# Attention of a DiT block: row maxima turned by VectorE and spread by ScalarE, output gathered channel-major by DMA and divided there

## The chip, the cores and the metric

The kernel runs on one core of a Trainium2 chip. The metric is device microseconds of one execution, lower is better. The core has a matrix engine (TensorE, PE in the profile, with its weight loads as PEld), VectorE (DVE), ScalarE (ACT), GpSimd (POOL) and SyncE (SP), which here only issues the DMAs, in the order in which they are written.

## The reference

One transformer block with modulation, over 32 samples of 256 tokens and 288 channels, all in float32:

```python
B, L, C = 32, 256, 288;  H = 16;  D = C // H;  FF = 4 * C      # D = 18, FF = 1152
ada = silu(c) @ W_ada + b_ada                                  # six vectors per sample
h = layernorm(x) * (1 + scale_msa) + shift_msa
q, k, v = split(h @ W_qkv + b_qkv)
attn = softmax(einsum('blhd,bmhd->bhlm', q * D ** -0.5, k), axis=-1)
o = einsum('bhlm,bmhd->blhd', attn, v).reshape(b, l, c)
x = x + gate_msa * (o @ W_proj + b_proj)
h = layernorm(x) * (1 + scale_mlp) + shift_mlp
x = x + gate_mlp * (gelu(h @ W_fc1 + b_fc1) @ W_fc2 + b_fc2)
```

## The kernel before

All engines run a list of steps (`PE_ORDER`, `ACT_ORDER`, `DVE_ORDER`, `POOL_ORDER`, `SYNC_ORDER`). An entry `("st", 0, 3)` is step `st`, for the sample whose number is that of the row plus 0, with index 3. `run` (L106) goes through the list once per row, so that in the middle of the kernel a row does each step once, for samples of different ages: the MLP works on sample k-2, the projection on k-1, the scores on k, the next QKV on k+1. The order is written out; semaphores set only how long a step waits. One row is one sample's worth of work, and there are 32 samples.

Precision: a float32 operand is split into a rounded part (`fp32r`) and a rest, and three products replace one. With 288 channels that is 7 matmuls for each output tile (`products`, L296).

Attention works in pairs of heads, 8 pairs a sample, 4 pairs a half:

- `qk` (L462) makes q and k, channels by tokens. ACT and DVE write the rounded part and the rest to `qst`. SP writes `qst` to DRAM (`qkw`, L365) and reads it back, 18 rows at a time, into `ql` and `kl` (`qkr`, L376, 24 reads a sample), which lines up high and low parts as one contraction of 108 rows.
- `s` (L484) computes the scores, tokens by keys, into two banks; DVE takes the row maxima (`head_max`, L814) and puts them into `mx`.
- `mt` (L502) turns the maxima of two pairs on PE (2 transposes); ACT copies four rows to `mxs` (L637); SP sends them to rows 108 and 109 of `ql` with 2 DMAs (`mx_out`, L396).
- `st` (L511) computes the scores again, keys by tokens, over 110 rows: the two extra rows subtract the maximum. 4 matmuls of 256 columns. ACT takes the exponential into `e` (L642).
- `pv` (L523), once per four heads (a quad), multiplies `e` with `ve`, 18 channels of v and a one for the sum per head. The result is channels by tokens, in four groups of 32 partitions. ACT copies it to `ots` (L650), `on` (L535) turns it on PE to tokens by channels, and DVE takes the reciprocal of the sums and multiplies (L823) into `onat`.
- `ot` (L541) turns `onat` on PE back to channels by tokens (6 transposes), ACT and DVE split it into `xh3`, `xl3`, `xr3`, and `proj` (L546) does the projection.

`lt`, `fc1`, `fc2`, `sum2` and the layer norms are the same before and after. POOL computes rests (`xl1`, `xl3`, `gl`) and additions. `xt` and `lt` are the PE transposes after the layer norms; they stay.

Of the kernel before, what the change touches and what calls it, by code (L numbers as in the profile page):

```python
# [26 lines left out]
KH = 2 * KS  # L27
KM = KH + 2
# [14 lines left out]
GROUPS = 4  # L43
MXW = 64 + 4 * GROUPS
READS = 8
# [3 lines left out]
A_USES = 2 + NT + 2 + 3  # L49
USE_PROJ, USE_LT, USE_FC1 = 2, 2 + NT, 4 + NT  # L50
B_USES = 2 + NT
USE_FC2 = 2
TURN_USES = 2 * QUADS
# [29 lines left out]

POOL_ORDER = [
    ("fc1", -2, 2), ("fc1", -2, 3), ("xt", 2, 0), ("fc1", -2, 4), ("proj", -1, 0), ("proj", -1, 1),
    ("ln2_stats", -1, 0), ("lt", -1, 0), ("sum2", -2, 0), ("bias", -1, 0), ("ln1_stats", 3, 0), ("sum2", -2, 1),
    ("fc1", -1, 0), ("fc1", -1, 1),
]

# [908 lines left out]
```

## Time and profile before

| | us |
|---|---|
| median of 3 runs | 1330.55 (1329.88 to 1333.33) |
| the profiled execution | 1333.92, its span 1332.1 |

| engine | busy us | share | instructions |
|---|---|---|---|
| PE | 1283.3 | 96% | 10995 |
| PEld | 1160.8 | 87% | 10995 |
| DVE | 884.9 | 66% | 2086 |
| ACT | 714.0 | 54% | 1163 |
| POOL | 480.2 | 36% | 522 |

Busy time counts an instruction from its start to its end. PE's instructions overlap, so what one of them costs is the distance from its start to the next one's start, which the chain of waits shows. The DMA engines were busy for about a third of the span. The first 120 us load weights and fill the pipeline of samples; the last 60 us drain it.

### The profile page before, as it was taken

The page shows a single profiled execution, that of the slowest core. Times are in us where ns is not written, and L with a number is a line of the kernel's source. Part 1 is how long each engine was busy: PE and PEld are TensorE (multiplying, and loading weights), DVE is VectorE, ACT ScalarE, POOL GpSimd, SP SyncE. Part 2 cuts the span into 40 slices and gives each one's busy share as a digit, 9 for nine tenths or more (in the row PEclk, how much of TensorE's full clock was granted, in tenths as well). Part 3 has the DMA queues.
Part 4 walks back from the last instruction along what each step waited for, and adds up shares of the span by engine and source line. Part 5 has one row for each costly group of instructions (what it writes and reads, how often), then busy time and mean ns, then how long its engine had stood idle before and what let it go on. Part 6 is the DMA issues. An engine that isn't in the chain of part 4 may idle for free.

```text
span 1332.1 us, 29243 instructions
## 1 busy us (share of the span) xinstructions
PE 1283.3 (96%) x10995; PEld 1160.8 (87%) x10995; DVE 884.9 (66%) x2086; ACT 714.0 (54%) x1163; POOL 480.2 (36%) x522
## 2 busy tenths in 40 slices
PE   6588999999999999999999999999999999999996
PEld 1477999999999999999999999999999999999886
DVE  5567666667667666666766667676667666766642
ACT  1345556556555555655556555555655555565541
POOL 2102343333334333333343333334333433433344
PEclk9998999999999999999999999999999999999998
DMA  7234333333333333433334343333424333332210
GB/s 233 87 122 136 103 109 112 105 116 122 115 115 103 108 115 105 127 112 116 106 103 125 95 130 112 117 103 105 124 92 131 112 119 108 101 114 85 82 47 18
DMA packets 82934, 146.27 MB, mean 110 GB/s; under 512 B 12486, under 2 KB 51496, under 8 KB 82796
## 3 DMA queue, kind: packets, MB, share of 16 engines
q1 hardware_dynamic: 82796, 144.40, 34.7%
q8 instruction: 90, 1.47, 0.5%
q14 instruction: 48, 0.39, 0.1%
HBM read 96.53 MB, written 47.30 MB: 108 GB/s over the span
## 4 chain that ended last, share of the span: by engine, by line
PE 94%; DVE 3%; ACT 1%; issue 1%; DMA 1%; POOL 0%; SPq 0%; POOLq 0%; ACTq 0%; DVEq 0%
PE x_bank L472 11%; PE a_bank L571 10%; PE turn_bank L530 9%; PE score_bank L497 9%; PE st_bank L519 9%; PE b_bank L571 8%; PE b_bank L585 6%; PE b_bank L587 6%; PE b_bank L586 6%; PE a_bank L552 5%; PE x_bank L480 5%; PE score_bank L507 2%; PE a_bank L450 2%; PE turn_bank L538 2%; PE x_bank L450 1%; PE a_bank L453 1%
## 5 line engine op out<-in xcount | busy, mean ns | idle before, releaser
L819 DVE TENSOR_REDUCE mx<-score_bank 128x2 f32<-128x512 f32 x512 | 337.9, 687 | 201.8 <-PE score_bank L497 199.4
L646 ACT ACTIVATE e<-st_bank 128x1024 f32<-128x1024 f32 x256 | 262.7, 1026 | 116.2 <-PE st_bank L519 112.1
L948 POOL TENSOR_TENSOR gl<-gl_raw,gh 128x512 fp32r<-128x512 f32 (+1 forms) x160 | 188.6, 1179 | 182.6 <-DVE gh L877 182.6
L585 PE MATMUL b_bank<-w,gh 128*128 128x288 f32 x576 | 176.5, 306 | 0.7 <-DVE tmp L883 0.6
L497 PE MATMUL score_bank<-kl,ql 108*128 108x256 f32 x1024 | 172.2, 290 | 1.1 <-ACT mxs L640 1.0
L519 PE MATMUL st_bank<-ql,kl 110*128 110x256 f32 x1024 | 170.2, 288 | 0.5 <-ACT e L646 0.5
L587 PE MATMUL b_bank<-w,gl 128*128 128x288 f32 x576 | 170.5, 296 | 0.0
L586 PE MATMUL b_bank<-w,gh 128*128 128x288 f32 x576 | 170.3, 296 | 0.0
L497 PEld LDWEIGHTS score_bank<-kl,ql 108*128 108x128 f32 x1024 | 142.1, 192 | 14.6 <-issue 14.5
L519 PEld LDWEIGHTS st_bank<-ql,kl 110*128 110x128 f32 x1024 | 140.5, 190 | 5.0 <-issue 1.3
L530 PE MATMUL turn_bank<-e,ve 128*32 128x256 f32 x2048 | 137.0, 385 | 0.1
L935 POOL TENSOR_TENSOR xl<-v,xh 128x512 fp32r<-128x512 f32 x32 | 41.3, 1292 | 213.7 <-DVE xh L869 213.7
L472 PE MATMUL x_bank<-xh,wq 128*128 128x256 f32 x640 | 106.8, 291 | 6.8 <-DVE qst L808 3.7
L585 PEld LDWEIGHTS b_bank<-w,gh 128*128 128x128 f32 x576 | 109.1, 189 | 1.3 <-DVE tmp L883 0.9
L571 PE MATMUL a_bank<-xh,w 128*128 128x256 f32 x640 | 105.7, 287 | 4.1 <-DVE xr L795 2.9
L586 PEld LDWEIGHTS b_bank<-w,gh 128*128 128x128 f32 x576 | 109.4, 190 | 0.0
L587 PEld LDWEIGHTS b_bank<-w,gl 128*128 128x128 f32 x576 | 108.8, 189 | 0.0
L627 ACT CAST qst<-x_bank 128x512 fp32r<-128x512 f32 (+1 forms) x96 | 49.3, 514 | 110.4 <-PE x_bank L472 109.6
L472 PEld LDWEIGHTS x_bank<-xh,wq 128*128 128x128 f32 x640 | 91.7, 198 | 8.5 <-issue 7.3
L640 ACT CAST mxs<-score_bank 4x256 fp32r<-4x256 f32 x128 | 46.5, 363 | 94.3 <-PE score_bank L507 92.6
L571 PEld LDWEIGHTS a_bank<-xh,w 128*128 128x128 f32 x640 | 88.0, 190 | 5.8 <-issue 5.8
L877 DVE CAST gh<-gl_raw 128x512 fp32r<-128x512 f32 (+1 forms) x160 | 85.3, 533 | 11.5 <-ACT gl_raw L679 11.4
(153 smaller groups left out, 2597.6 us busy)
## 6 DMA issues: line engine op xcount, KB each, us to landing
qk_rows<-qst SPq DMA_DIRECT2D x128, 256.0 KB, 2.5
ql<-qk_rows SPq DMA_DIRECT2D x384, 72.0 KB
kl<-qk_rows SPq DMA_DIRECT2D x384, 72.0 KB
gate<-gates SPq DMA_DIRECT2D x32, 432.0 KB, 4.7
xin<-in_x SPq DMA_DIRECT2D x32, 288.0 KB, 3.0
x<-in_x SPq DMA_DIRECT2D x32, 288.0 KB, 3.2
out<-x SPq DMA_DIRECT2D x32, 288.0 KB, 3.1
qk_rows<-qst SPq DMA_DIRECT2D x32, 128.0 KB, 4.7
```

What stands on the lines that cost most here:

```text
L472: last = nc.tensor.matmul(x_bank[:, k * L:(k + 1) * L], wa[:, c * P:(c + 1) * P], xa, start=(i == 0), stop=(i == len(pr) - 1))
L497: last = nc.tensor.matmul(score_bank[i][:, t * L:(t + 1) * L], ql[0:KH, slot, i, j % HP, t * P:(t + 1) * P], kl[0:KH, slot, j % HP, :], st ...
L519: last = nc.tensor.matmul(st_bank[:, i, u, :], kl[0:KM, slot, j % HP, u * P:(u + 1) * P], ql[0:KM, slot, i, j % HP, :], start=True, stop=True)
L530: last = nc.tensor.matmul(turn_bank[VB * c:VB * (c + 1), 0:L], ve[:, b % 2, u, 4 * q + c, :], e[:, 2 * (q % 2) + c // 2, c % 2, u, :], sta ...
L571: last = nc.tensor.matmul(bank[:, (f % 2) * L:(f % 2 + 1) * L], wa[:, f * P:(f + 1) * P], xa, start=(i == 0), stop=(i == len(pr) - 1))
L585: nc.tensor.matmul(b_bank[:, 0:C], gh[:, cols], w2[:, 0, f, :], start=(f == 0), stop=False)
L586: nc.tensor.matmul(b_bank[:, 0:C], gh[:, cols], w2[:, 1, f, :], start=False, stop=False)
L587: last = nc.tensor.matmul(b_bank[:, 0:C], gl[:, cols], w2[:, 0, f, :], start=False, stop=(f == NF - 1))
L646: nc.scalar.activation(e[:, j % 4, :, :, :].rearrange("p i u l -> p (i u l)"), st_bank[:, :, :, :].rearrange("p i u l -> p (i u l)"), ACT. ...
L819: nc.vector.tensor_reduce(mx[:, b % 2, :, col:col + 1], score_bank[i][:, :].rearrange("p (t l) -> p t l", t=NT), AX.X, ALU.max).then_inc(s ...
L877: nc.vector.tensor_copy(gh[:, cols], g[:, cols]).then_inc(g_hi, 1)
L948: nc.gpsimd.tensor_tensor(gl[:, cols], g[:, cols], gh[:, cols].bitcast(F32), ALU.subtract).then_inc(g_lo, 1)
```

## The change

The change takes three kinds of PE transposes away and moves their work to DVE, ACT and DMA.

- **Maxima.** DVE writes the maxima of four pairs (a half) so that its own transpose in blocks of 32 (`mt`, now on DVE) puts them into rows. ACT then spreads them with 8 copies of 4 partitions (`mb`) straight into rows 64 to 67 of `ql`. `kl` has a -1 in the row of the pair concerned and 0 in the others. The two reads of zeros a sample (`qkr` with `m == 12`) clear these rows of `ql` before `s`, which now contracts over the same 122 rows as `st`. `mt` on PE, the copy to `mxs` and the 8 DMAs of `mx_out` go.
- **Scores, keys by tokens.** `st` uses 2 matmuls of 512 columns in place of 4 of 256.
- **Output.** `pv` is done once per eight heads. ACT copies both quads' results to `on` in one go; SP writes them to DRAM (`ow`, 4 DMAs) and reads them back as packed channels (`or`, 6 DMAs), 7 heads in each of two tiles and 2 heads in a third. The sums go on their own: gathered over 64 partitions (`sr`, 2), reciprocal on DVE (`rcp`), out to DRAM (`sw`, 2), read back repeated 18 times (`rr`, 6). DVE multiplies (`om`), ACT rounds (`oh`), POOL and DVE take the rest (`ol`), `proj` contracts over 126 rows. `on` and `ot` on PE go.
- The five lists are written anew.

The core of the diff (`...` marks what is left out):

```diff
 def st(b, j):
-    if j % 2 == 0:
-        pe.wait_ge(mx_rows[gr % 2], 32 * (2 * b + gr // 2 + 1))
+    if j % HP == 0:
+        pe.wait_ge(mx_rows, HALVES * b + j // HP + 1)
     wait(pe, e_ready, PAIRS * b + j)
-    for i in range(2):
-        for u in range(NT):
-            last = nc.tensor.matmul(st_bank[:, i, u, :], kl[0:KM, slot, j % HP, u * P:(u + 1) * P],
-                                    ql[0:KM, slot, i, j % HP, :], start=True, stop=True)
+    for u in range(NT):
+        last = nc.tensor.matmul(st_bank[:, u, :, :], kl[0:KM, slot, j % HP, u * P:(u + 1) * P],
+                                ql[0:KM, slot, :, j % HP, :], start=True, stop=True)
...
-def mt(b, gr):                       # PE: 2 transposes, 4 times a sample
-def on(b, q):                        # PE: 2 transposes, 4 times a sample
-def ot(b, n):                        # PE: 4 and 2 transposes, once a sample
...
+def mb(b, half):                     # ACT
+    act.wait_ge(mx_turned, HALVES * b + half + 1)
+    rows = ql[MXR:MXR + HP, slot, :, :, :].rearrange("p i j (t a x) -> p i j t a x", t=NT, x=VB)
+    for t in range(NT):
+        for a in range(P // VB):
+            src = mxt[VB * a:VB * a + HP, half, :, t, :].unsqueeze(2).broadcast_to([HP, 2, HP, VB])
+            last = nc.scalar.copy(rows[:, :, :, t, a, :], src)
+    last.then_inc(mx_rows, 1)
...
+def mt(b, half):                     # DVE
+    for i in range(2):
+        dve.wait_ge(s_max[i], PAIRS * b + HP * (half + 1))
+    wait(dve, mx_rows, HALVES * (b - 1) + half + 1)
+    nc.vector.transpose(mxt[:, half].rearrange("p i t v -> p (i t v)"),
+                        mx[:, half].rearrange("p i t v -> p (i t v)")).then_inc(mx_turned, 1)
+def rcp(b, half):                    # DVE
+    dve.wait_ge(sums_loaded[half], 16 * (b + 1))
+    wait(dve, rc_stored[half], 16 * b)
+    nc.vector.reciprocal(rc[part, :], sums[part, :]).then_inc(rc_ready, 1)
...
+def sum_read(b, half):               # SP
+    sp.wait_ge(turn_drained, HALVES * b + half + 1)
+    sp.dma_start(sums[P // 2 * half:P // 2 * (half + 1), :], ...).then_inc(sums_loaded[half], 16)
+def rc_write(b, half):
+    sp.wait_ge(rc_ready, HALVES * b + half + 1)
+    sp.dma_start(r_dram[b % 2, half]..., rc[...]).then_inc(rc_stored[half], 16)
...
 def proj(b, t):
-    pe.wait_ge(a_drained, A_USES * b + USE_PROJ + t)
-    pr = products(xh3, xl3, xr3, wp)
+    pe.wait_ge(o_lo, b + 1)
+    pe.wait_ge(o_rem, b + 1)
+    wait(pe, a_drained, A_USES * b + USE_PROJ + t)
+    pr = products(oh, ol, orem, wp, OT, OREM)
```

How the order moves, at the places that matter. First PE, in the middle of a row. Before, around the end of the MLP's first layer and the start of the second (`L538` is `on`, `L507` `mt`, `L450` `ot` and `xt`):

```order
L571 MATMUL b_bank<-xr,w 128x256
L538 MATMUL turn_bank<-ident,ots 128x128 x2
L507 MATMUL score_bank<-ident,mx 68x128 x2
L571 MATMUL a_bank<-xh,w 128x256 x4
L571 MATMUL a_bank<-xl,w 128x256 x2
L571 MATMUL a_bank<-xr,w 128x256
```

and now, with `L655` for `fc1`, `L610` for `st` and `L599` for `s`:

```order
L655 MATMUL b_bank<-xr,w 128x256
L655 MATMUL a_bank<-xh,w 128x256 x4
L655 MATMUL a_bank<-xl,w 128x256 x2
L655 MATMUL a_bank<-xr,w 128x256
L610 MATMUL st_bank<-ql,kl 128x512 x2
L599 MATMUL score_bank<-kl,ql 128x256 x4
```

The transposes between the blocks of `fc1` are gone, all five blocks of `fc1` are issued before the row's first `st`, and an `st` is 2 instructions.

Second ACT, at the exponentials after the GELUs. Before (`L657` and `L659` are `ot`, `L652` `pv`, `L640` `mt`):

```order
L646 ACT_TABLE_LOAD
L646 ACTIVATE e<-st_bank 128x1024
L657 CAST xh<-a_bank 128x512
L618 ACTIVATE v<-x_bank,mod 128x256 x2
L659 CAST xr<-a_bank 96x256
L646 ACTIVATE e<-st_bank 128x1024
L652 COPY ots<-turn_bank 128x256
L640 CAST mxs<-score_bank 4x256
```

Now the later half of a row, from the fourth exponential on (`L738` is `st`, `L731` `mb`, `L720` `v`, `L748` `pv`):

```order
L738 ACTIVATE e<-st_bank 128x1024
L731 CAST ql<-mxt 4x8x32 x8
L720 COPY ve<-x_bank 128x16x18
L748 COPY on<-turn_bank 128x512
L738 ACTIVATE e<-st_bank 128x1024
L702 ACTIVATE xl_raw<-x_bank,mod 128x256 x2
```

The small copies come in two blocks of 8, and the copy of the `pv` result stands behind such a block.

Third SP's queue, over the stretch in which the output goes out and comes back. Before it held the reads of q and k and the maxima:

```order
L392 DMA kl<-qk_rows 18x1024
L402 DMA ql<-mxs 1x2x256 x2
L392 DMA kl<-qk_rows 18x1024 x2
L373 DMA qk_rows<-qst 128x2x256 x2
L392 DMA ql<-qk_rows 18x1024 x5
L402 DMA ql<-mxs 1x2x256 x2
```

Now (`L460` is `sw`, `L451` `sr`, `L445` `ow`, `L494` `or`, `L481` `rr`, `L407` `qkw`, `L435` `qkr`):

```order
L460 DMA r_rows<-rc 64x32
L451 DMA sums<-on 64x1x32
L445 DMA o_rows<-on 4x32x256 x2
L383 DMA xin<-in_x 128x576
L494 DMA ol_raw<-o_rows 126x1x256
L498 DMA out<-x 128x576
L481 DMA rcb<-r_rows 126x1x256
L407 DMA qk_rows<-qst 128x2x256
L460 DMA r_rows<-rc 64x32
L494 DMA ol_raw<-o_rows 126x1x256
L494 DMA orem_raw<-o_rows 36x1x256 x2
```

The writes and reads of the output and of the sums stand between the reads of q and k of one sample and the writes of q and k of the next, and the queue waits for a reciprocal of DVE twice in a row. A row issues 55 DMAs, where it issued 41.

## Rows read from the trace of the kernel before

**Rows 1.** The page: busy time of each engine, and the chain's shares by engine.

```profile
PE 1283.3 (96%) x10995; PEld 1160.8 (87%) x10995; DVE 884.9 (66%) x2086; ACT 714.0 (54%) x1163; POOL 480.2 (36%) x522
...
PE 94%; DVE 3%; ACT 1%; issue 1%; DMA 1%; POOL 0%; SPq 0%; POOLq 0%; ACTq 0%; DVEq 0%
```

**Rows 2.** Stretches: length, busy PE, PEld, DVE, ACT, POOL, clock, DMA share, GB/s.

```profile
200.00:1250.00 1050.00, 1049.70 (x9286) 965.08 (x9278) 722.88 (x1727) 599.16 (x977) 396.08 (x431) 1.00 0.36 112
...
1200.00:1238.70 38.70, 38.70 (x343) 35.54 (x343) 24.48 (x55) 20.54 (x33) 12.58 (x13) 1.00 0.33 105
...
1290.00:1310.00 20.00, 13.87 (x91) 12.75 (x90) 8.79 (x23) 3.52 (x7) 8.95 (x10) 0.91 0.00 1
```

**Rows 3.** The chain of waits over one row: start us, us, what.

```profile
601.23 0.48 PE score_bank L497 x4
601.70 1.00 PE turn_bank L530 x16
602.70 1.12 PE x_bank L480 x7
603.83 1.65 PE a_bank L571 x14
...
606.44 0.93 PE x_bank L480 x7
...
609.04 0.22 PE turn_bank L538 x2
...
610.45 0.13 PE b_bank L586
...
611.99 0.44 PE a_bank L450 x4
...
615.01 0.22 PE a_bank L453 x2
...
640.39 1.00 PE turn_bank L530 x16
```

**Rows 4.** Groups by line (two stretches): busy, mean ns of one, idle before.

```profile
L640 ACT CAST mxs<-score_bank 4x256 fp32r<-4x256 f32 x128 | 46.5, 363 | 94.3 <-PE score_bank L507 92.6
...
L652 ACT COPY ots<-turn_bank 128x256 f32<-128x256 f32 x42 | 15.7, 373 | 4.1 <-PE turn_bank L530 4.1
...
L657 ACT CAST xh<-a_bank 128x512 fp32r<-128x512 f32 x11 | 6.4, 582 | 0.0
...
L842 DVE TENSOR_TENSOR xl<-a_bank,xh 128x512 fp32r<-128x512 f32 x11 | 7.6, 691 | 3.9 <-ACT xh L657 3.9
...
L827 DVE RECIPROCAL rc<-turn_bank 128x8 f32<-128x8 f32 x42 | 8.4, 201 | 9.5 <-PE turn_bank L538 9.5
...
L830 DVE TENSOR_TENSOR onat<-turn_bank,rc 128x144 f32<-128x144 f32 x43 | 13.2, 307 | 1.5
...
L930 POOL TENSOR_TENSOR xl<-v,xh 128x512 fp32r<-128x512 f32 x11 | 14.1, 1283 | 34.7 <-DVE xh L800 34.7
```

**Rows 5.** SP's issues in order of time: start us, us, what, count.

```profile
612.54 0.43 SPq L362 DMA_DIRECT2D gate<-gates  x1
...
613.40 1.07 SPq L373 DMA_DIRECT2D qk_rows<-qst  x2
...
623.02 1.23 SPq L402 DMA_DIRECT2D ql<-mxs  x2
...
629.36 0.78 SPq L392 DMA_DIRECT2D kl<-qk_rows  x2
630.19 2.46 SPq L373 DMA_DIRECT2D qk_rows<-qst  x2
```

**Rows 6.** The page: DMA issues, KB each, median us to landing.

```profile
qk_rows<-qst SPq DMA_DIRECT2D x128, 256.0 KB, 2.5
...
qk_rows<-qst SPq DMA_DIRECT2D x32, 128.0 KB, 4.7
```

**Rows 7.** SP's waits from 600 to 1010 us: us in total, times, longest.

```profile
SPq L382 <- DMA qk_rows<-qst: 62.8, 21, 4.9
```

More of the change, by code:

```diff
@@ L26 @@
 KS = 3 * D
-KH = 2 * KS
-KM = KH + 2
+MXR = 64
+HB = MXR + PAIRS // 2
+KM = HB + KS
 VB = 32
@@ L260, in dit_block @@
                                      (w_fc1, b_fc1, w1, w1_raw, FF)):
+            rows, rem = (OT, OREM) if w is w_proj else (P, KRB)
             for k in range(2):
-                loads.append(("full", w, None, raw[:, 2 + k, :], dst[:, k, :], dst[:, 2 + k, :], n, k))
-            loads.append(("rem", w, bias, g[0:KRB, at:at + n], dst[0:KRB, 4, :], None, n, 2))
+                loads.append(("full", w, None, raw[0:rows, 2 + k, :], dst[0:rows, k, :], dst[0:rows, 2 + k, :], n, k))
+            loads.append(("rem", w, bias, g[0:rem, at:at + n], dst[0:rem, 4, :], None, n, 2))
+            if w is w_proj:
+                wp_rem_raw = g[:, at:at + n]
             at += n
@@ new lines, in sum_read @@
+            def sum_read(b, half):
+                wait(sp, rc_ready, HALVES * (b - 1) + half + 1)
+                sp.wait_ge(turn_drained, HALVES * b + half + 1)
+                sp.dma_start(sums[P // 2 * half:P // 2 * (half + 1), :],
+                             on_sb[D:P:VB, :, :].rearrange("c q l -> c (q l)").rearrange("c (x i) -> c x i", i=VB)
+                             ).then_inc(sums_loaded[half], 16)
+            def rc_write(b, half):
+                sp.wait_ge(rc_ready, HALVES * b + half + 1)
+                if half == 0 and b >= 2:
+                    sp.wait_ge(rc_rows[b % 2], 16 * O_READS * (b // 2))
+                sp.dma_start(r_dram[b % 2, half].rearrange("c q (x i) -> (c q x) i", i=VB),
+                             rc[P // 2 * half:P // 2 * (half + 1), :]).then_inc(rc_stored[half], 16)
@@ new lines, in o_read @@
+            def o_read(b, n):
+                if n == 0:
+                    wait(sp, a_full, A_USES * (b - 1) + USE_PROJ + NT)
+                    sp.wait_ge(o_stored[0], 32 * (b + 1))
+                    if b == 0:
+                        sp.wait_ge(consts, N_CONSTS - 1)
+                if n == 1:
+                    sp.wait_ge(o_stored[1], 32 * (b + 1))
+                to, h0, nh = o_place(ol_raw, orem_raw, n)
+                heads = o_dram[b % 2].rearrange("f c q v l -> (f c q) v l")[:, 0:D, :]
+                sp.dma_start(to, heads[h0:h0 + nh]).then_inc(o_rows[b % 2], 16)
@@ L411, in _ @@
                 load_weights(i)
+            sp.wait_ge(consts, N_CONSTS - 1)
+            for jj in range(HP):
+                row = slice(MXR + jj, MXR + jj + 1)
+                sp.dma_start(kl[row, :, jj, :].bitcast(F32),
+                             tmp2[row, 0, 0:L].unsqueeze(1).broadcast_to([1, SLOTS, L])).then_inc(kl_rows, 16)
+            sp.dma_start(zero_dram, ql[MXR:MXR + HP, 0, :, :, :].rearrange("p i j l -> p (i j l)").bitcast(F32)
+                         ).then_inc(zeros_stored, 16)
             fetch_x(1)
@@ L499, in s @@
                                                 start=True, stop=True)
                     last.then_inc(s_full[i], 1)
-            def mt(b, gr):
-                for i in range(2):
-                    pe.wait_ge(s_max[i], PAIRS * b + 2 * gr + 2)
-                for t in range(NT):
-                    last = nc.tensor.transpose(mt_ps[0:68, t * P:(t + 1) * P],
-                                               mx[:, b % 2, t, 4 * gr:4 * gr + 68], ident[:, :])
-                last.then_inc(mt_full, 1)
@@ new lines, in st, with pv @@
+                last.then_inc(st_full, 1)
+            def pv(b, half):
+                pe.wait_ge(e_ready, PAIRS * b + HP * (half + 1))
+                if half == 0:
+                    pe.wait_ge(x_drained, X_USES * (b + 1))
+                wait(pe, turn_drained, HALVES * b + half)
+                for q in range(2):
+                    for u in range(NT):
+                        for c in range(4):
+                            last = nc.tensor.matmul(turn_bank[VB * c:VB * (c + 1), q * L:(q + 1) * L],
+                                                    ve[:, b % 2, u, 8 * half + 2 * c + q, :],
+                                                    e[:, c, u, q, :],
+                                                    start=(u == 0), stop=(u == NT - 1))
+                last.then_inc(turn_full, 1)
@@ L839, in ot @@
-            def ot(b, n):
-                dve.wait_ge(o_hi, 2 * b + n + 1)
+            def mt(b, half):
[7 more added lines that the diff above has]
+                wait(dve, rc_stored[half], 16 * b)
+                part = slice(P // 2 * half, P // 2 * (half + 1))
+                nc.vector.reciprocal(rc[part, :], sums[part, :]).then_inc(rc_ready, 1)
```

305 lines of the change are left out of this document (179 added, 126 removed), and 34 rows, old and new, of tables (ACT_ORDER, DVE_ORDER, PE_ORDER, POOL_ORDER).

## The prediction

> **What bounds the kernel now.** I read the page's busy times first, then the stretches, then the chain of waits over one row, and last the groups of the engines that take over the work. The page says PE 96% and a chain that runs 94% through PE [rows 1]. The stretches say where: from 200 to 1250 us PE is busy for 1049.70 of 1050 us at full granted clock, and only near the end does it leave gaps (13.87 of 20 us, clock 0.91) [rows 2]. DVE is busy there for 722.88/1050 = 69% and ACT for 57%. So the middle is one engine deep, and what a step costs there is its share of PE's time.
>
> A busy PE need not be a full one, so I take the chain's own distances. The first quad's `pv` of one row starts at 601.70 and the same step of the next row at 640.39: a row is 38.69 us [rows 3]. Its steps add up to that. `s` and `st` are 8 each at 0.48 = 7.7. `pv` is 4 at 1.00, and the block behind it takes 1.12 where the same block elsewhere takes 0.93, so 4 x 1.19 = 4.8. `qk` is 2.5 x 1.66 = 4.15, `v` and `proj` 4 x 0.93 = 3.7, `fc1` 4.5 x 1.66 = 7.5, `fc2` 54 x 0.133 = 7.2 (its row is rounded to 0.13; 288 columns against 256 at 0.119 give 0.133). `mt` is 4 x 0.22, `on` 4 x 0.22, and `ot`, `xt`, `lt` are 0.44 + 0.22 each. Sum 38.8, against 38.69: no idle time is left over, and a removed PE step gives its full price.
>
> The Trainium skill would read this otherwise: its page Perfetto Trace Analysis (Identifying the Most-Contended Engine) holds that busy matmuls say little and that the busy share of the weight loads is the measure. Here that is 87% [rows 1], and by it about an eighth of PE's time would be slack. But a block of 7 with 288 columns takes 0.93 and one with 256 takes 1.65/2 = 0.83, with weights of the same width [rows 3], so the moving columns set the pace; by this the trace does not agree.
>
> **What the change removes on PE.** Per row: 8 transposes of `mt`, 8 of `on`, 6 of `ot`, each 0.11: 22 x 0.11 = 2.42 us. `pv` comes in 2 pieces instead of 4, and two of the four slow starts behind it go: 2 x 0.19 = 0.38. `st` streams as many columns with half as many instructions. Nothing, if time goes by columns; at most the fixed part of 16 matmuls, which I bound by 0.119 less 256 columns at 2.4 GHz (0.107) = 0.012 each, 0.2 us. The rows at 256 and 288 columns (0.119, 0.133) lie nearer to pure proportion, so I take 0.1. `s` and `proj` contract over other numbers of rows; `s` at 108 and `st` at 110 rows cost the same 0.48, as do blocks with a remainder of 98 rows, so that is 0. In all 2.9 us, and the row's floor is 35.8 us (bounds 35.7 to 35.9).
>
> **What it adds elsewhere.** ACT is at 0.57 x 38.69 = 22.1 us a row. It loses 4 x 0.363 + 4 x 0.373 + 0.58 + 0.37 = 3.9 and gains 16 small copies, 2 copies of 512 columns at 0.58, and 0.58 + 0.37 for the rounding [rows 4]. The small copies are the nearest thing to L640 (4 partitions, 256 elements, 363 ns): 5.8 us, bounded by 0.2 each, for an instruction that only starts (as the small reciprocal), and 0.58, for one of 512 columns, so 3.2 to 9.3. ACT comes to 26 us (24 to 30) of 35.8. DVE is at 26.6; it loses about 3.5 (`on` 4 x 0.51, `ot` 1.1, small copies 0.4) and gains 2 transposes of 128 elements (between 0.2 and 0.69, I take 0.3, near L830), 2 reciprocals at about 0.3, 0.69 + 0.42 for the product and 0.42 for the rest: 25.8. POOL gains 1.28. None of them becomes the bound by its sum.
>
> SP issues 55 DMAs a row instead of 41. At the prices of [rows 5]: 26 reads at 0.39, 5 writes of q and k at 0.53 to 1.23 (0.8), 4 others at 0.43, 4 small ones at 0.61, 4 writes of the output at 0.53, 12 reads at 0.43: 10.1 + 4.0 + 1.7 + 2.4 + 2.1 + 5.2 = 25.5 us, where it was 20. To this come two waits a row for landed q and k, 62.8/21 = 3.0 each [rows 7]: 31.5 of 35.8. The DMA engines carry 1.3 MB more in a row on top of 4.5 MB (144.40 MB over 32): the share goes from 0.36 [rows 2] to about 0.36 x 1.3 x 38.7/35.8 = 0.51.
>
> **The paths that have to fit.** All in PE time between the steps, by [rows 3].
> - From `s` 7 to `st` 4 stand 2 `v`, 2 `proj`, one `st`, one `pv` of eight heads: 4 x 0.93 + 0.46 + 2.19 = 6.4 us. Needed: two maxima 1.4, transpose 0.3, 8 copies 2.9 = 4.6. Slack 1.8. The same for the first half: 8.0 against 4.6.
> - From `pv` of the second half to `proj`: 5 blocks of `fc1`, 3 of `qk`, 6 `s`, 4 `st`, 2 parts of `fc2`, 1 `v`: 19.8 us. Needed: copy 0.6, three DMA legs (issue 0.6 + landing 2.5 [rows 6], again 3.1, six reads 2.6 + 2.5), reciprocal 0.3, product 0.7, rounding 0.6, POOL 1.3 = 14.8. Slack 5. With landings of 4.7 each it is 21.4, 1.6 too long.
> - From `qk` 1 to the next sample's `s` 0: 19.7 us. Needed: cast and rest 1.3, about 3 of queueing on ACT behind `mb` and the GELUs, two writes 2.5, landing 2.5, 13 reads 5.1, landing 2.5 = 16.9. Slack 2.8. Before, this path had most of a row more.
>
> The Trainium skill, DMA: Bandwidth & Descriptors (Anatomy of one DMA), puts about 2.0 us on a small DMA, most of it the receipt of the last write, most of all into HBM. This estimate would make the three legs 6 us plus issues, and the middle path about 13 us; no row here shows a transfer of so few bytes landing.
>
> DVE's queue also waits now for DMA: `rcp` stands ahead of the third maximum of a sample, so late sums hold `s` back.
>
> I expect the slacks to hold mostly, with 0.4 us of PE waits a row (bounds 0 and the 1.6 above). Row: 36.2, a gain of 2.5 us over 31 full rows = 77 us. **The ends** cost something: in the drain only about 7.5 + 2.4 = 9.9 us of MLP lie between the last `pv` and its `proj`, for a path of 14.8, so 5 us of idle PE; at the start four pairs instead of two must be scored before the first `st`, 1 us. Plus 6 (0 to 12). Span 1332.1 - 77 + 6 = 1261. The profiled execution took 1333.92, 1.8 over its span and 3.4 over the median, so **1260 us** against 1330.55.
>
> **The rivals.**
> - *Waits take half of the gain.* One of the three paths is late in each row, most likely q and k or the output, since both pass SP's queue. At the 1.6 us worked out above the row is 37.4, the gain 31 x 1.3 = 40 us: 1295. For it: slacks of 2 to 5 us against landings that already vary from 2.5 to 4.7. Against: PE is in order, so a late row shifts the others along and the slack grows back.
> - *SP's queue becomes the bound, and the kernel is slower.* The place is the stretch of output and sum DMAs. The 22 new issues have prices from 0.39 to 1.23 (the write pair at 630.19). The rest of SP's row is 15.1 plus 6 of waits, so the queue binds from 0.67 us per new issue, and decides for slower from (38.7 - 21.1)/22 = 0.80. At 0.9 a row is 40.9, 2.2 longer: 1330 + 68 + 6 = 1405 us. For it: the same write took 0.53 in one place and 1.23 in another, so issues slow when the queue is full, and each of the new waits (for a reciprocal, for landed sums) stops all reads behind it. Against: reads are issued at 0.39 to 0.43.
> - *PE is not what the gain is paid in.* If the freed time is only refilled with waits on the scores (DVE's maxima at 0.69 each follow every `s`), the row stays at 38.7: 1333. DVE's 69% speaks against it.
> - *Everything hides*, ends too: 35.7 x 31 gives a gain of 93, 1237.
>
> **Chances.** Forecast (1243 to 1275) 0.62; waits take part (1275 to 1320) 0.20; everything hides (below 1243) 0.06; row unchanged 0.03; SP bound, slower 0.09. A measurement of this kernel can tell about 0.3%, 4 us, from no change: faster 0.88, same 0.02, slower 0.10. The range 1240 to 1305 leaves out about 0.03 below and 0.15 above.
>
> **What would show it.** Right: the `pv` of one half starts about 36.2 us after the same one in the row before; PE busy for over 98% of the middle at full clock; no group of transposes but `xt` and `lt`; small copies near 0.36; ACT near 26 and DVE near 26 us a row. Wrong: PE idle before `proj`, `s` or `st` in sum over 1 us a row, put down to POOL `ol`, to the DMAs into `ql`, or to ACT's copies; SP issuing without a pause; `rcp` on DVE waiting for `sums` with maxima queued behind it; 1.2 GHz stretches in the middle.

## The result: 1.8% slower, and the profile after

The changed kernel takes 1354.91 us (median of 4 runs, 1351.16 to 1361.93) against 1330.56 of before in the same comparison (1329.88 to 1333.33): a ratio of 1.018, 95% interval 1.015 to 1.021. The forecast was 1260 with a range to 1305, so both the sign and the range were wrong. The profiled execution has a span of 1350.1 us, against 1332.1.

The page of the changed kernel, as in [rows 1] busy time by engine and the chain's shares by engine and by line:

```profile
PE 1227.3 (91%) x9779; PEld 1081.7 (80%) x9779; DVE 940.7 (70%) x1929; ACT 871.3 (65%) x1483; POOL 530.6 (39%) x557
...
PE 29%; issue 17%; DMA 17%; SPq 13%; POOL 12%; DVE 7%; ACT 4%; POOLq 0%; DVEq 0%; ACTq 0%
```

PE did become lighter: 1227.3 us busy instead of 1283.3, 1216 instructions fewer. But the chain that was 94% PE is now 29% PE. Its largest line is `DMA r_rows<-rc 10%`, a transfer of 8 KB: the reciprocals on their way to DRAM.

Where the time lies is best seen between the stores of the output. I cut both traces at the store of the first sample and at that of the 28th, 27 rows apart. The first row here is before, the second after (columns as in [rows 2]):

```profile
176.54:1221.18 1044.64, 1044.64 (x9242) 961.14 (x9238) 720.75 (x1725) 596.25 (x973) 395.48 (x430) 1.00 0.36 112
```

```profile
185.04:1225.87 1040.83, 992.12 (x8204) 891.37 (x8203) 770.80 (x1588) 727.87 (x1242) 437.94 (x457) 0.99 0.48 147
```

| stretch | before | after | difference | foreseen |
|---|---|---|---|---|
| to the first store | 176.5 | 185.0 | +8.5 | about +1 |
| 27 rows | 1044.6 | 1040.8 | -3.8 | -67.5 |
| from there to the end | 110.9 | 124.2 | +13.3 | -10 (four rows) +5 |

A row went from 38.69 to 38.55 us. So what PE gave back was eaten in the row itself, and the two ends made the kernel slower. PE's busy time fell by 52.5 us over the 27 rows (1.94 a row) and 48.7 us of idle time came in its place (1.80 a row). PE's waits in that stretch, total us, times, longest:

```profile
PE st_bank L610 <- ACT e L738: 41.4, 27, 2.5
PE a_bank L636 <- DVE tmp L964: 3.2, 3, 1.7
```

It is one wait, exactly once in each of the 27 rows: `st` for its bank, which ACT's exponential empties. The prediction had idle time before `st` among its signs of being wrong, but put it down to ACT's copies of the maxima, not to an exponential. The other engines' waits tell what stands behind it; ACT, DVE and SP's queue in turn:

```profile
ACT oh L754 <- DVE ol_raw L946: 58.6, 27, 3.1
```

```profile
DVE rc L939 <- DMA sums<-on: 56.8, 27, 3.7
...
DVE ol_raw L946 <- DMA rcb_rem<-r_rows: 47.8, 27, 2.7
```

```profile
SPq L416 <- DMA qk_rows<-qst: 117.7, 52, 5.4
SPq L450 <- ACT on L748: 59.7, 27, 3.5
SPq L498 <- POOL x L1077: 33.6, 28, 2.7
SPq L481 <- DMA r_rows<-rc: 26.9, 25, 2.2
```

All occur about once or twice a row. (The wait of `rc` for the sums is that of the first half's reciprocal, at 604.82 in the row below; the second half's, at 611.77, starts without a wait.) The chain over one row puts them in order (start us, us, what; the eight heads' `pv` had ended at 607.86, and the copy L748 ran from 607.93 to 608.52):

```profile
611.78 0.78 POOL x L1077
...
612.57 0.36 SPq L498
...
613.03 0.82 SPq L481
...
613.95 0.47 SPq L407
...
614.49 4.57 DMA r_rows<-rc
...
619.07 0.79 SPq L481
...
621.70 0.77 SPq L481
...
622.52 2.38 DMA rcb_rem<-r_rows
...
624.92 0.70 DVE ol_raw L946
...
625.64 0.03 ACT oh L754
...
626.17 1.03 ACT e L738
...
627.24 0.74 PE st_bank L610 x2
...
628.46 1.76 PE x_bank L582 x7
```

Read from below. PE's `st` at 627.24 waits for the exponential at 626.17. That one is late though its scores were there at 624.2: in ACT's list `oh(-1,0)` stands ahead of it, and `oh` waits for the product of the output with the reciprocals. The product waits for the last of the reads of reciprocals, those for the landing of the write of the reciprocals, and that write was issued only at 614.49 although the reciprocals were there at 612.12: it stands in SP's queue behind a store, a read and a write of q and k. The store itself waited for POOL's last addition of the MLP until 612.56, 0.4 us longer than the reciprocals took; this is the branch that the profile's chain follows, and where its 12% of POOL come from. Both branches go back to PE at nearly the same place. The sums come from `pv` (605.93 to 607.86), and `pv` of a second half needs the exponentials. POOL's addition stands in POOL's list behind work on the transposes of `lt`, a step just ahead of that `pv` in PE's list (605.62). So the loop is closed. One row is once around it, and PE only runs along. The last line shows the rest of the price: behind the gap the block of 7 that takes 0.93 in [rows 3] takes 1.76. The granted clock of that stretch (its column is the third from the right) is half of full speed, the level of 1.2 GHz, after 1.84 us in which PE had stood still:

```profile
628.30:630.30 2.00, 2.00 (x10) 2.00 (x9) 1.82 (x4) 0.95 (x2) 0.00 (x0) 0.53 0.73 281
...
632.00:634.00 2.00, 2.00 (x16) 1.99 (x16) 0.66 (x2) 1.93 (x6) 0.87 (x2) 1.00 0.70 197
```

### The profile page after: what moved, and what is told of

The parts are those of the page before. It is cut to its first block, busy times and chain, and to the rows that moved or that the text cites. A ratio compares the mean times of both kernels' runs of the same rounds, so it can differ in the third digit from the quotient of the medians.

```text
span 1350.1 us, 27363 instructions
## 1 busy us (share of the span) xinstructions
PE 1227.3 (91%) x9779; PEld 1081.7 (80%) x9779; DVE 940.7 (70%) x1929; ACT 871.3 (65%) x1483; POOL 530.6 (39%) x557
## 4 chain that ended last, share of the span: by engine, by line
PE 29%; issue 17%; DMA 17%; SPq 13%; POOL 12%; DVE 7%; ACT 4%; POOLq 0%; DVEq 0%; ACTq 0%
DMA r_rows<-rc 10%; SPq L481 9%; PE st_bank L610 5%; PE turn_bank L622 5%; PE a_bank L636 5%; DMA rcb_rem<-r_rows 5%; PE x_bank L582 4%; POOL x L1071 3%; POOL xl L1042 3%; POOL xl L1047 3%; ACT e L738 2%; DMA gate<-gates 2%; SPq L494 2%; POOL x L1077 2%; SPq L407 2%
## 5 line engine op out<-in xcount | busy, mean ns | idle before, releaser
L922 DVE TENSOR_REDUCE mx<-score_bank 128x2 f32<-128x512 f32 x512 | 331.7, 680 | 60.8 <-PE score_bank L599 57.4
L738 ACT ACTIVATE e<-st_bank 128x1024 f32<-128x1024 f32 x256 | 262.1, 1024 | 52.4 <-PE st_bank L610 46.2
L610 PE MATMUL st_bank<-ql,kl 122*128 122x512 f32 x512 | 178.4, 430 | 60.1 <-ACT e L738 54.8
L731 ACT CAST ql<-mxt 4x256 fp32r<-4x256 f32 x512 | 206.2, 403 | 12.0 <-DVE mxt L931 5.2
L599 PEld LDWEIGHTS score_bank<-kl,ql 122*128 122x128 f32 x1024 | 154.4, 196 | 28.3 <-issue 11.3
L599 PE MATMUL score_bank<-kl,ql 122*128 122x256 f32 x1024 | 173.9, 293 | 2.1 <-DVE mx L922 1.9
L610 PEld LDWEIGHTS st_bank<-ql,kl 122*128 122x128 f32 x512 | 81.8, 196 | 86.2 <-ACT e L738 65.6
L622 PE MATMUL turn_bank<-e,ve 128*32 128x256 f32 x2048 | 125.3, 386 | 0.7 <-ACT e L738 0.7
L1047 POOL TENSOR_TENSOR xl<-xl_raw,xh 128x512 fp32r<-128x512 f32 x32 | 41.3, 1290 | 198.4 <-DVE xh L977 198.4
L1059 POOL TENSOR_TENSOR x<-tmp,x 128x288 f32<-128x288 f32 x64 | 51.3, 802 | 157.6 <-DVE tmp L964 157.6
L655 PE MATMUL a_bank<-xh,w 128*128 128x256 f32 x640 | 104.5, 285 | 8.4 <-DVE xr L898 3.9
L655 PEld LDWEIGHTS a_bank<-xh,w 128*128 128x128 f32 x640 | 88.3, 191 | 12.0 <-issue 6.1
L622 PEld LDWEIGHTS turn_bank<-e,ve 128*32 128x32 f32 x2048 | 60.4, 110 | 46.0 <-issue 11.6
```

Source lines behind the costliest of these rows:

```text
L599: last = nc.tensor.matmul(score_bank[i][:, t * L:(t + 1) * L], ql[0:KM, slot, i, j % HP, t * P:(t + 1) * P], kl[0:KM, slot, j % HP, :], st ...
L610: last = nc.tensor.matmul(st_bank[:, u, :, :], kl[0:KM, slot, j % HP, u * P:(u + 1) * P], ql[0:KM, slot, :, j % HP, :], start=True, stop=True)
L622: last = nc.tensor.matmul(turn_bank[VB * c:VB * (c + 1), q * L:(q + 1) * L], ve[:, b % 2, u, 8 * half + 2 * c + q, :], e[:, c, u, q, :], s ...
L655: last = nc.tensor.matmul(bank[:, (f % 2) * L:(f % 2 + 1) * L], wa[:, f * P:(f + 1) * P], xa, start=(i == 0), stop=(i == len(pr) - 1))
L731: last = nc.scalar.copy(rows[:, :, :, t, a, :], src)
L738: nc.scalar.activation(e[:, j % 4, :, :, :].rearrange("p u i l -> p (u i l)"), st_bank[:, :, :, :].rearrange("p u i l -> p (u i l)"), ACT. ...
```

## The experiments

Each kernel is the changed one with the edit shown, unless it says otherwise. Rows and waits are taken between the second and the 27th store, 25 rows. Times are set against the kernel before, run on the same chip.

**e1: the write of the second half's reciprocals goes ahead of the store.**

```diff
-    ("or", -1, 0), ("store", -3, 0), ("rr", -1, 0), ("qkw", 1, 0), ("sw", -1, 1), ("or", -1, 1),
+    ("or", -1, 0), ("sw", -1, 1), ("store", -3, 0), ("rr", -1, 0), ("qkw", 1, 0), ("or", -1, 1),
```

> Only SP's list changes: the DMA that writes the second half's reciprocals to DRAM (sw) stands ahead of the store of an older sample and of one read and one write, behind which it was issued at 614.49 though the reciprocal was ready at 612.12. Theory A (the output's way through SP and DRAM is what is too long: it ends in a rounding copy on ACT that stands in front of the second exponential, and PE waits for that exponential 1.5 us a row, and runs slow after it): the way gets about 2 us shorter, the wait for the exponential goes below 0.3 us a row, the clock in the middle rises to 1.00, a row goes from 38.55 to 36.0 to 36.9 us, the time from 1355 to 1290 to 1312. Rival B (ACT with 70% load and the copies of the maxima is itself what is late, the output's way only waits beside it): the row stays over 38.0, the time over 1338.

Measured: 1327.62 us, ratio 0.997 (0.995 to 0.999), row 37.59, between the bands of the two theories. One entry of SP's list is worth 1.0 us a row and 27 us of the whole. The wait of `st` fell only from 1.5 to 1.22 us a row, and the chain of this kernel has another last link:

```profile
631.26 5.35 DMA o_rows<-on
636.63 0.78 SPq L494
...
639.33 0.78 SPq L481
```

The write of 128 KB of output takes 5.35 us to land, and the ten reads behind it take 6.8 us to issue (636.63 to 643.45).

**e2: the reads of the divisor wait for nothing.** They fetch rows of x, so the divisor is another. (The wait for `rc_stored[1]` goes too.)

```diff
-                    sp.wait_ge(rc_stored[0], 16 * (b + 1))
-                src = r_dram[b % 2].rearrange(...)[h0:h0 + nh].unsqueeze(1)...
+                src = x[b, h0:h0 + nh, 0:L].unsqueeze(1)...
```

> The six reads of the reciprocals (rr) read rows of the input x of the same size and do not wait for the reciprocals to be in DRAM; the sums are still gathered, inverted and written. The division is by other numbers, so the output is not the reference's. Theory A: the two legs of the sums fall out of the way to the product, the wait for the second exponential goes to 0, a row is 36.0 to 36.6 us, the time 1285 to 1300, and the drain at the end is shorter by some 5 us of its 13 us excess. Rival B: the row stays over 38.0, the time over 1335.

Measured: 1331.85 us, ratio 1.000 (0.998 to 1.001), row 37.85, wait of `st` 1.26 a row. That is between the two theories again: taking the whole trip of the reciprocals away brings no more than issuing it in time did in e1. The branches of the loop are nearly equally long; below one lies the other. In some rows the chain of this trace goes through the landing of the output (5.42 us from 480.66). In others it has no landing but the last: the store waits for POOL's last addition until 634.03, and the ten reads behind it go out one after the other from 636.39 to 643.35.

**e3: the `oh` copies stand one exponential later in ACT's list.**

```diff
-    ("oh", -1, 0), ("st", 0, 1), ("qk", 1, 2), ("oh", -1, 1), ("st", 0, 2), ("v", 1, 0), ...
+    ("st", 0, 1), ("qk", 1, 2), ("oh", -1, 0), ("st", 0, 2), ("oh", -1, 1), ("v", 1, 0), ...
```

> Only ACT's list changes: the two rounding copies of the output (oh) stand one exponential later each. Theory A: the output's way is as long as before (product at about 24.9 us of a row that begins at 600), but the second exponential no longer waits; the wait moves in part to the projection, about 1 us a row. A row of 37.0 to 38.0 us, the time 1312 to 1340. If the wait for the exponential is only a symptom and the projection is as late as before, the whole comes back there: 1350 to 1360.

Measured: 1345.86 us, ratio 1.011 (1.006 to 1.015), row 38.40. The wait for the exponential is gone from PE's list and the row is hardly shorter. (The profiled execution, 1352.0 us, was the longest of the four; by the medians e3 is 9 us shorter than the changed kernel.) PE's new waits, and the largest of its weight loads (PEld):

```profile
PE x_bank L582 <- DVE qst L911: 14.5, 18, 1.3
PE score_bank L599 <- DVE mx L922: 5.5, 11, 1.0
```

```profile
PEld score_bank L599 <- DVE mx L922: 19.1, 40, 1.4
```

DVE's list has the same knot as ACT's: the product that waits for the DMA stands ahead of maxima and of `qst`, so its lateness reaches PE by that way. These waits are about half of the old one (20.0 of 37.5 us in 25 rows); another 12 are in PE's own busy time, 930.9 us where it was 919.0. Mostly it is the late product that costs, not the engine that hands it on.

**e4: the maxima are spread by 4 copies of 512 elements a half instead of 8 of 256.**

```diff
-                for t in range(NT):
-                    for a in range(P // VB):
-                        src = mxt[VB * a:VB * a + HP, half, :, t, :].unsqueeze(2).broadcast_to([HP, 2, HP, VB])
+                for a in range(P // VB):
+                    src = mxt[VB * a:VB * a + HP, half, :, :, :].unsqueeze(2).broadcast_to([HP, 2, HP, NT, VB])
```

> The maxima are spread by 4 copies of 512 elements for each half instead of 8 of 256. At 0.58 each (the cast of 512 columns) 2.4 us for 3.3, so ACT has 1.8 us less a row. Theory A: ACT's first exponential is at most 1 us earlier, but the second still waits for the output, whose way has no such copy in it; the copy of the second pv of a row is not moved: 38.0 to 38.6 us a row, 1340 to 1357. Rival B: ACT is what is late, the row falls by 1 us or more, 1320 or less.

Measured: 1343.66 us, ratio 1.009 (1.006 to 1.012), row 38.45. ACT got 1.5 us a row lighter (674.6 us over 25 rows in the changed kernel, 637.8 here), the row 0.1 shorter, and `st` waits as long as before (38.0 us in 25 rows, 37.5 in the changed kernel). So ACT's load is not what holds the row. It is not quite nothing: the medians are 11 us apart, 0.8%, the two intervals do not overlap, and the profiled execution (1350.12) was the longest of seven, so its row hides some of that.

**e5: nothing of the trip is waited for.** Output and divisor are both read from rows of x; the writes, the gather of the sums and the reciprocals still run. (The waits for the other half go too.)

```diff
-                    sp.wait_ge(rc_stored[0], 16 * (b + 1))
-                    sp.wait_ge(o_stored[0], 32 * (b + 1))
-                heads = o_dram[b % 2].rearrange("f c q v l -> (f c q) v l")[:, 0:D, :]
+                heads = x[b, 0:D * nh, 0:L].rearrange("(h v) l -> h v l", v=D)
```

> The changed kernel, but the reads of the output's rows and of the reciprocals' rows fetch rows of x instead and wait for nothing written in the same sample (the writes, the gather of the sums and the reciprocals still run), so what is multiplied is other data. Theory A (the kernel loses its gain in one loop: copy of the second half, trip through DRAM, product, oh copy ahead of the second exponential): nothing in this trip is waited for any more, so the wait of st for the second exponential (1.53 us a row in the changed kernel) goes to under 0.3, and with it the slow restart behind it (0.9); row 35.8 to 36.6 against 38.55; the drain rows, which were the trip itself, get 2 to 3 us shorter each; time 1265 to 1300. Rival B (SP's queue or DVE's own load sets the row, whatever the trip does): row 37.5 or more, since issues and DVE work are as many; the wait moves to score_bank or x_bank. Rival C (the middle recovers but the start keeps +8.5 us): the row as A, the first store still near 180.

Measured: 1294.38 us, ratio 0.971 (0.969 to 0.974), row 36.78. Stretch and PE's largest wait:

```profile
216.11:1135.51 919.40, 910.18 (x7602) 818.09 (x7601) 716.49 (x1476) 675.96 (x1150) 406.74 (x425) 1.00 0.51 155
```

```profile
PE st_bank L606 <- ACT e L734: 3.8, 5, 1.2
```

As many DMAs and as much DVE work as in the changed kernel, and 1.8 us a row less: the loss sits in the trip, not in the number of DMAs. Not all of the 1.8 is waiting, though. The reads of x also cost SP less to issue than those of the output (medians 0.55 and 0.36 us, where it was 0.79 and 0.53), some 1.2 us a row, and most of these reads stand in the same trip. e8 below reaches the same row, 36.78, with the reads at their old price and two more DMAs, so dearer reads need not cost it. The row came out 0.2 above the expected band. PE itself is busy for 910.18/25 = 36.4 us a row, and that, not a wait, is the missing part: my floor of 35.8 was too low. In the changed kernel it was 36.75, so the slow restarts cost about 0.35 a row. The first store is at 179.4 instead of 185.0, so 5.7 of the 8.5 us at the start were the same loop; from the 28th store to the end it still takes 121.3.

**e6: wide writes, on top of e1.** Heads are placed so that one write covers 128 whole rows in DRAM; the sums are gathered by two DMAs a half.

```diff
-                sp.dma_start(o_dram[b % 2, half, :, q], on_sb[:, q, :]).then_inc(o_stored[half], 16)
+                sp.dma_start(o_dram[b % 2, half, q].rearrange("c v l -> (c v) l"), on_sb[:, q, :]).then_inc(...)
```

> On top of e1 (sw ahead of the store). The heads of a half lie in DRAM so that each write of the output covers 128 whole rows of one block instead of 4 x 32 rows with gaps; the sums are gathered by two DMAs a half instead of one. Theory A (the write of the output is slow, 5.35 us, for its shape: 4 x 32 x 256 goes over 4 engines, 128 rows over 16): it lands in about 3 us; om comes 2 us earlier, the wait for the second exponential falls from 1.22 to 0.2 to 0.5 a row, row 36.3 to 37.2 against 37.59, time 1295 to 1318. Rival B (the landing is a receipt in DRAM or queueing behind other traffic, which a wider write does not shorten): landing stays above 4.5, row 37.6, and two more issues a row cost 0 to 0.5 us: 1325 to 1335. Rival C (the path through the sums and reciprocals is then the last one): landing falls, row only 37.3 or so, and om waits for rcb_rem behind rr reads.

Measured: 1304.18 us, ratio 0.979 (0.976 to 0.983), row 37.08, `st`'s wait 17.1 us in 25 rows. That is inside theory A's range, with a longer wait than it had (0.68 us a row). The same 128 KB now land in 1.9 us in the median (the line has min, median, max):

```profile
DMA to landing us min/median/max: 1.7/1.9/4.8
```

More issues a row, and a shorter row: rival B is out. Rival C is half right, since the chain now ends in the reads of the reciprocals again (the landing at 711.21, behind reads issued from 705.07 on). No landing stands between the reciprocals and it any more: from 702.34 to 711.21 SP issues 13 DMAs one after the other, 8.9 us. The price of an issue is itself a part of the loop.

```profile
702.34 0.52 SPq L461
...
705.07 0.79 SPq L495
...
711.21 2.24 DMA rcb_rem<-r_rows
713.47 0.70 DVE ol_raw L947
```

**e7: two semaphores, on top of e1.** The reads into the main tiles signal their own and go first.

```diff
-    ("or", -1, 1), ("or", -1, 2), ("or", -1, 3), ("or", -1, 4), ("rr", -1, 1), ("rr", -1, 2), ...
+    ("or", -1, 1), ("or", -1, 2), ("rr", -1, 1), ("or", -1, 3), ("or", -1, 4), ("rr", -1, 2), ...
-                sp.dma_start(to, src).then_inc(rc_rows[b % 2], 16)
+                sp.dma_start(to, src).then_inc((rc_rows if n < 2 else rc_rest)[b % 2], 16)
```

> On top of e1. The reads of the output and of the reciprocals signal two semaphores, one for the part in the main tiles and one for the rest, and the ones of the main part are issued first; om of the main tiles waits for its own only. Theory A (om waits 6 us for nine reads issued one after the other, of which it needs three): om and the oh copies come 2 to 4 us earlier, the wait for the second exponential goes under 0.4 a row, row 36.2 to 37.0 against 37.59, time 1290 to 1312. Rival B (the second product, of the rest, holds oh(1) or DVE instead): the wait moves to oh(1) and the third exponential, row 37.4 or more, 1322 to 1335.

Measured: 1317.34 us, ratio 0.989 (0.985 to 0.992), row 37.43. The row is rival B's, the time between the two: the wait for the exponential is gone altogether (30.5 us in 25 rows in e1), but 12.4 us come back at the bank of `proj`, and PE's busy time is 8.4 us longer, which no run explains.

```profile
PE a_bank L640 <- DVE tmp L970: 12.4, 15, 1.9
```

**e8: e1, e6 and e7 together.**

> e1, e6 and e7 together. Theory A (one loop, whose parts add up): the second exponential is never late, row 35.9 to 36.6, time 1278 to 1300, faster than before by 2 to 4%. Rival B (below about 37 us something else binds: DVE at 28.6 us a row with its in-order waits, or SP's queue with two more issues): row 36.8 to 37.4, not better than the better one of e6 and e7, and the idle time of PE is put to score_bank or x_bank.

Measured: 1283.69 us, ratio 0.965 (0.961 to 0.969), faster than before by 3.5%, in theory A's range. e1 brought 27 us over the changed kernel, e6 another 23, and the split wait, worth 10 on top of e1, another 20 on top of e6: what one cure brings depends on what the others have left. The profiled execution was the longest of the four (1292.5 us); its row is 36.78. No exponential is waited for, and nearly all of PE's idle time is `PE a_bank L641 <- DVE tmp L971: 11.0, 12, 2.0`, where DVE waits for the gates:

```profile
DVE tmp L971 <- DMA gate<-gates: 24.1, 17, 2.8
```

**e9: the load of residual and gates ahead of three writes of q and k, on top of e8.**

```diff
-    ("rr", -1, 5), ("qkw", 1, 1), ("qkw", 1, 2), ("qkw", 1, 3), ("res", -1, 0), ("qkr", 1, 0), ...
+    ("rr", -1, 5), ("res", -1, 0), ("qkw", 1, 1), ("qkw", 1, 2), ("qkw", 1, 3), ("qkr", 1, 0), ...
```

> On top of e8: the load of the residual and the gates goes ahead of the last three writes of q and k instead of behind them. In e8 the only wait of PE left in the middle is proj's second half for the bank, held by DVE's product with the gates (0.44 us a row), and DVE waited there for the gates. Theory A: that wait goes, the row falls from 36.75 to 36.3 (PE's own work), time 1268 to 1278. Rival B: the q and k writes come 1 us later and s waits for the kl rows instead, row 36.7 or more, 1283 or more.

Measured: 1339.35 us, ratio 1.005 (1.003 to 1.008), row 38.27. Theory A was right about the gates and wrong about the row: rival B, and stronger than I had thought. Some 0.9 us of issues moved (0.47 and 0.42 below) cost 1.5 us a row.

```profile
PE score_bank L604 <- DMA ql<-zeros: 43.1, 25, 4.3
PE a_bank L641 <- DVE tmp L971: 0.6, 1, 0.6
```

Its chain over a row is the second loop of this kernel, through the third path of the prediction:

```profile
605.21 1.24 DVE mx L927 x2
...
607.25 0.36 DVE rc L944
607.63 0.52 SPq L465
...
617.31 0.47 SPq L397
617.83 0.42 SPq L398
...
618.77 4.72 DMA qk_rows<-qst
623.61 0.30 SPq L437
...
627.90 4.38 DMA ql<-zeros
632.32 0.74 PE score_bank L604 x4
```

A maximum, the reciprocal that is queued behind it on DVE, the write of reciprocals on SP, ten reads, the two loads, the write of q and k and its landing of 4.72 us behind 720 KB of loads (the 256 KB writes landed in 4.6 us in the median, in e8 in 3.1), twelve reads, the scores, and 10 us of PE's and DVE's lists up to the next such maximum at 642.66. The output's reads and the reads of q and k share one queue, so what is issued or waited for on behalf of the one holds the other.

**e10: e9 with e4's four copies.**

> On top of e9: the maxima are spread by 4 copies of 512 elements a half instead of 8 of 256, which took 1.5 us a row off ACT in e4. Theory A (with the loop's path short enough, ACT at 27 of 36.3 us a row limits nothing): row as in e9 within 0.15; start and end together 0 to 3 us shorter; ratio to e9 within 0.4%. Rival B (ACT's queue still delays an exponential or the maxima here and there, as 37.5 us of waits in 25 rows did in the changed kernel): row 0.3 us shorter than e9.

Measured: 1334.74 us, ratio 1.002 (0.999 to 1.005), row 38.09. A row 0.18 us shorter and 0.3% of the whole, between the two theories in the row and within what the two intervals tell apart. ACT's load limits little in this loop too.

**e11: e9 with the write of the reciprocals back behind the store.**

> e9 with the write of the second half's reciprocals back behind the store, the first reciprocal read and a q/k write, where the changed kernel has it. Theory A (a loop: the write of the reciprocals was the last link only while it was issued 2 us late; the wide write and the split wait do not shorten that link): the reads of the reciprocals wait again, the wait for the second exponential or for proj comes back at 0.3 to 1.2 us a row, row 36.8 to 37.5, time 1285 to 1310. Rival B (the slack won by the other two covers it): row 36.3 to 36.6, as e9.

Measured: 1408.96 us, ratio 1.059 (1.058 to 1.061), row 40.75. Far outside both theories. The place is e9's:

```profile
PE score_bank L604 <- DMA ql<-zeros: 75.3, 25, 4.3
```

SP waits 43.1 us in 25 rows for the landing of the reciprocals (L486) and 11.6 for POOL's addition (L503), at places where the rest of the queue, the q and k writes among it, is held up. These 2.2 us a row on the second loop go with a row 2.5 longer.

**e12: e8, with gates and residual in the other order, nothing moved past q and k.**

```diff
+                sp.dma_start(gate[:, b % 2], gates_dram[b]...).then_inc(gate_loaded[b % 2], 16)
                 sp.dma_start(x1[:, b % 2], x[b].rearrange("(p t) c -> p t c", t=NT)).then_inc(res_loaded[b % 2], 16)
-                sp.dma_start(gate[:, b % 2], gates_dram[b]...).then_inc(gate_loaded[b % 2], 16)
```

> On top of e8, and in place of e9's move: the two loads of the same step change places, gates first and residual second; nothing is moved past the writes or reads of q and k. In e8 PE's one wait left in the middle was 0.44 us a row for the bank that DVE's product with the gates holds, and the gates landed 4.9 us after an issue that stood 0.5 us behind the residual's. Theory A (e9 lost 1.5 us a row because 720 KB of loads went ahead of the writes of q and k, not because the gates came early): the gates land 1 to 2 us earlier, the wait falls under 0.15 a row, q and k are untouched, row 36.3 to 36.5 against 36.75, time 1270 to 1281. Rival B (the gates' landing is set by the traffic of the q and k writes and reads around it, not by their own place): row 36.6 to 36.8, 1281 to 1288. Rival C (any shift of these loads disturbs the reads of q and k): waits of s for ql<-zeros, 1290 or more.

Measured: 1284.46 us, ratio 0.965 (0.963 to 0.968), the same as e8. Its profile looks better than e8's: row 36.46, `PE a_bank L641 <- DVE tmp L971: 5.4, 9, 1.2`, first store at 176.9. But that execution took 1281.9 us and the profiled one of e8 1292.5, while both kernels have executions near 1282 and near 1293. Only the medians compare, and they say B; the gates landed no sooner (5.4 us in the median, in e8 4.9). Rival C is out: e9's loss came from the place of the loads, not from touching them.

## Why the prediction was wrong, by its own steps

**What PE gives up.** Foreseen 2.9 us a row, floor 35.8. Measured, with the waits taken out, 36.4 (e5; in e12 903.08/25 = 36.1). Between starts of the steps in order, before and in e8, the transposes went from 3.5 to 1.2 us a row, `pv` from 4.00 to 3.86 and `s` with `st` from 8.16 to 8.03. That is 2.3 to 2.6. The term was mis-sized by 0.3 to 0.6, some 15 us in all; `pv` itself gave 0.14 of the 0.38 put on it and the slow starts behind it. The transposes gave their price, 2.3 of 2.42, so the eighth of slack in PE that the busy share of the weight loads would suggest was not there. Streaming 512 columns in one instruction saves next to nothing: an `st` takes 0.46 to 0.47 in e6's chain, where it took 0.48.

**The path from `pv` to `proj`.** This step failed, in two ways. First the place: I measured its slack to `proj`, 19.8 us after `pv`, because `proj` is what reads the result. But the first thing that waits is the copy `oh` in ACT's list, and behind it in that list stands the second exponential, which has to empty the bank for the row's third `st`; PE reaches that `st` about 17.5 us after `pv` (607.86 to 625.4). The prediction asks of SP and of `rcp` on DVE what stands behind the waiting instruction, and not of ACT. The need up to that `st`, by my own prices, is 12.2 + 0.7 + 0.6 + 1.0 = 14.5 (up to the product, product, rounding, exponential), so this alone would have left 3.0 us.

Second the length. From the end of `pv` to the product I had 12.2 us and the trace of after has 17.1 (607.86 to 624.92). The first leg fits: the reciprocal starts 3.2 us after the copy. (DVE was busy with maxima and `qst` until 611.73, so when the sums landed is not seen.) Then the write of the reciprocals stood 2.4 us in SP's queue, 0.4 of them behind the store's wait for POOL, a term that the sum did not have at all; it took 4.57 us to land, where issue and landing were put at 3.1 together (median 3.8 for its landing); and the reads with the last landing took 5.8 instead of 5.1, since a read of this kind costs 0.44 to 0.79 us to issue, not 0.43. 17.1 + 0.7 for the product + 0.5 to the start of the exponential + 1.0 for it = 19.4, with the small gaps between, against 17.5: late by the 1.84 us that this row shows. e1 and e5 test both ends of this: 1.0 us a row for the place in the queue, 1.8 for the whole trip, cheaper reads included.

**The wait that takes the place.** I gave the rows 0.4 us of waits and reasoned that PE, being in order, lets the slack grow back. It can't where the late step is a link of a loop that passes through PE: then each row is as late as the one before. The loop sets the row, here at 38.55, and by chance at nearly the old 38.69. "Row unchanged" had 0.03, for another reason.

**From `s` to `st`, the maxima.** Held. The eight copies took 0.403 us each, 3.31 in all (0.363 foreseen), ACT 27.0 us a row (26), the transpose on DVE 0.31 (0.3). PE's matmuls wait for this path nowhere, and e4 shows that ACT's load has little to do with the wait. DVE had 28.6 us a row, not 25.8: the product of the rest took 1.16 us where 0.42 was taken, and some operations that did not change got longer too (`xn` of 128x64 0.79 and 0.55 us in the mean, where it was 0.31). Why was not tested.

**From `qk` to the next `s`.** Not late in the changed kernel, but its slack was thin, as foreseen with 2.8: in e9 and e11 it became the bound. The rival that makes SP's queue the bound named the right queue and the wrong reason. SP's issues sum to 27.2 us a row in the changed kernel (25.5 foreseen), and in e8 to 27.8 with a row of 36.78, so their sum does not bind. What costs is a stretch of them inside a loop (8.9 us in e6), and the waits in the queue in front of work that another loop needs.

**The ends.** Foreseen +6, measured +21.8. In the last row PE waits 8.4 us for POOL's `ol` (`PE a_bank L636 <- POOL ol L1052: 8.4, 1, 8.4`), where I had 5 more than before. The path from the last `pv` to POOL's `ol`, put at 14.8, took 18.6 (1293.28 to 1311.84), 4.75 of them for the landing of the output. The start, +1 in the sum, cost 8.5; it is 2.3 in e8 and 0.4 in e12, so most of it was the loop once more. Of the end's 13.3 us some 7 to 9 are left in e12 and e8 (118.1 and 119.8 against 110.9). That the rest was the loop is not shown: e1, with the shorter row, has a longer end than the changed kernel (127.1 against 124.2).

What stays open: why the end is still some 10 us longer than before with nothing of the trip waited for (e5: 121.3 against 110.9), what makes single executions of e8 and e12 differ by 0.9%, and why PE's and DVE's busy time grow in some runs without more work. The part of the change on the maxima was not run by itself.

## What to carry to other kernels

A slack is measured to the first instruction that waits, in every engine's list, and includes what stands behind that instruction there; the reader of the result is often not the one that comes first. When a change adds a round trip, draw the loop through all queues (producer, waits inside SP's list, landing, consumer, what is queued behind the consumer, back to the producer), and price it at once around: here it was longer than the bound engine's own row, so it was the row, and no slack elsewhere gave it back. Issues of a queue count in that length one by one. Then look for the shortest cures: one list entry was worth 27 us here, a write's shape 23, a split semaphore 20 (10 without the new shape), and together they turned 1.8% slower into 3.5% faster. A move in a shared queue can lengthen another loop, as e9 did.

## What the runs showed of the hardware that I had not expected

- The shape of a write sets its landing. 128 KB from 128 partitions took 5.35 us into four blocks of 32 rows with gaps between, and 1.9 us in the median into 128 rows without (e1, e6); the issue fell from 0.54 to 0.38 us. This fits the Trainium skill, DMA: Bandwidth & Descriptors (Why a DMA increments its semaphore by 16 and not by 1): a transfer is spread over the largest number of engines up to 16 that divides the slowest dimension on both sides. For 4 and 128 that gives 4, for 128 and 128 it gives 16. No row here shows the engines of one transfer, but the two times are on the side that the rule says. The gaps went together with the four blocks, so their share is not separated. A transfer right behind the writes gained as well: `xin`, 288 KB, landed in 5.5 us in the median of e1 and in 3.0 in e6.
- 8 KB took 2.7 to 5.6 us to land in DRAM, 3.8 in the median, longer than 256 KB in [rows 6] and than the 2.0 of the prediction's estimate for a small DMA; it was always issued with other transfers in the queues.
- Reads of the output and of the divisor cost SP 0.44 to 0.79 us each to issue, those of q and k 0.32.
- The time of one kernel varied by 1.0% between executions for e3 (1338.7 to 1352.0) and by 1.3% for e9 (1329.39 to 1346.04), but by only 0.4% for e1 (1325.1 to 1330.87), all with a loop through DRAM as the bound. The kernel before, whose middle hangs on PE, varied by 0.6% in 22 executions (1328.47 to 1336.0). What makes the difference is not shown.
